# A router product with its operands exchanged: adapter stage of a two-layer mixture-of-experts kernel

## What is computed

```python
# _L0_cond_ref: an adapter chosen by language, then a layer norm
h = relu(einsum('bsh,bha->bsa', x, W1[lang]) + b1[lang])       # a = 64
adapted = einsum('bsa,bah->bsh', h, W2[lang]) + b2[lang]
y = layernorm(x + adapted) * gamma[lang] + beta[lang]
# _L0_ffn_ref: expert-choice routing, 8 experts take 128 of 512 rows each
logits = einsum('bsh,eh->bse', y, Wg)                          # 8 logits a row
Sm = swapaxes(softmax(logits, axis=-1), 1, 2)
G, I = top_k(Sm, 128)
# gather rows I, expert FFN (256 -> 1024 -> 256), scale by G, add back at I
...
```

## Time and profile before

| | us |
|---|---|
| median of three runs | 1123.51 |
| lowest and highest | 1120.33, 1127.12 |
| the profiled execution | 1121.38 |
| its span, first to last instruction | 1119.6 |
| TensorE matmuls busy | 955.4 (85%) |
| TensorE weight loads busy | 680.7 (61%) |
| VectorE busy | 746.9 (67%) |
| ScalarE busy | 460.5 (41%) |
| POOL busy | 662.7 (59%) |
| mean granted clock of TensorE | 0.929 |

### The profile page before, as it was taken

One profiled execution on the slowest core, in us unless ns is written; L12 is line 12 of the kernel. 1 busy time (PEld: TensorE's weight loads), 2 busy tenths in 40 slices (PEclk: granted clock), 3 DMA queues, 4 the chain that ended last, 5 costly groups with the idle time before them and its releaser, 6 DMA issues.

```text
span 1119.6 us, 15008 instructions
## 1 busy us (share of the span) xinstructions
PE 955.4 (85%) x4616; PEld 680.7 (61%) x4616; DVE 746.9 (67%) x1529; ACT 460.5 (41%) x835; POOL 662.7 (59%) x494
## 2 busy tenths in 40 slices
PE   4988899999999999988269889888687799899960
PEld 2664499989998999863125445444454465556640
DVE  3547466666766676524778999999974787777620
ACT  1221354455445554443446565757321232232320
POOL 2113434455544654315999989999940477777870
PEclk9768999999999999998699999999876999999995
DMA  5949534354443442134212832244258599996557
GB/s 177 283 150 343 140 62 95 83 118 93 95 109 88 89 97 45 20 60 110 95 39 77 260 129 89 95 137 129 96 170 296 163 267 269 255 260 154 91 75 155
DMA packets 89783, 155.48 MB, mean 139 GB/s; under 512 B 12072, under 2 KB 70128, under 8 KB 86576
## 3 DMA queue, kind: packets, MB, share of 16 engines
q1 hardware_dynamic: 48112, 91.27, 25.0%
q0 software_dynamic: 25104, 39.86, 20.2%
q10 hardware_dynamic: 16496, 23.49, 6.4%
HBM read 119.56 MB, written 43.42 MB: 146 GB/s over the span
## 4 chain that ended last, share of the span: by engine, by line
issue 12%; POOL 12%; DVE 10%; PE 7%; DMA 6%; DVEq 3%; ACT 1%; POOLq 1%; ACTq 0%
DVE wide L1270 5%; DMA odd_rows<-ys,slots 3%; POOL xg L717 3%; POOL wide L639 2%; PE bank L1656 2%; POOL wide L631 2%; POOL out L724 2%; POOL odd_rows L724 2%; DMA xg<-z_rows,slots 1%; DMA out<-ys,slots 1%; DVEq L1309 1%; PE bank L1733 1%; PE bank L1723 1%; PE bank L1743 1%; ACT wide L891 1%
## 5 line engine op out<-in xcount | busy, mean ns | idle before, releaser
L631 POOL TENSOR_TENSOR wide<-wide 128x1024 f32<-128x1024 f32 x64 | 156.4, 2457 | 30.9 <-issue 30.9
L1270 DVE TENSOR_TENSOR_SCAN wide<-bank,wide 128x512 f32<-128x512 f32 x128 | 149.3, 1210 | 22.7 <-POOL wide L631 22.7
L867 ACT ACTIVATE h_raw<-bank,b 128x512 f32<-128x512 f32 x128 | 87.9, 688 | 168.2 <-PE bank L1629 165.6
L1207 DVE TENSOR_TENSOR h_lo<-h_raw,h_hi 128x512 fp32r<-128x512 f32 x128 | 87.3, 692 | 92.2 <-ACT h_hi L871 88.8
L1644 PE MATMUL bank<-w_hi,h_hi 128*128 128x256 f32 x512 | 144.3, 282 | 0.1
L1644 PE MATMUL bank<-w_hi,h_lo 128*128 128x256 f32 x512 | 142.3, 278 | 0.0
L1644 PE MATMUL bank<-w_lo,h_hi 128*128 128x256 f32 x512 | 142.3, 278 | 0.0
L605 POOL DMA_INDIRECT x_rows<-ob,put x64 | 110.3, 1723 | 28.3 <-issue 16.0
L639 POOL TENSOR_TENSOR wide<-wide 128x1024 f32<-128x1024 f32 x46 | 108.4, 2357 | 11.5 <-issue 8.1
L891 ACT ACTIVATE wide<-wide,blend 128x512 f32<-128x512 f32 x128 | 84.1, 716 | 61.1 <-POOL wide L631 57.4
L1629 PE MATMUL bank<-ex_hi,w_hi 128*128 128x512 f32 x256 | 99.5, 389 | 2.1 <-issue 2.1
(11 more groups left out here) (235 smaller groups left out, 2019.9 us busy)
## 6 DMA issues: line engine op xcount, KB each, us to landing
wide<-in_mwp SPq DMA_DIRECT2D x40, 512.0 KB
wide<-m_rows SPq DMA_DIRECT2D x16, 1024.0 KB, 4.8
w1s<-in_fW SPq DMA_DIRECT2D x8, 1024.0 KB, 5.0
w2s<-in_fW SPq DMA_DIRECT2D x8, 1024.0 KB
own<-in_mwp SPq DMA_DIRECT2D x15, 512.0 KB
z_rows<-zrow SPq DMA_DIRECT2D x8, 640.0 KB, 7.1
head<-in_mwp SPq DMA_DIRECT2D x9, 512.0 KB
xT<-in_xT ACTq DMA_DIRECT2D x8, 512.0 KB, 4.4
```

The costliest lines, as they stand in the source:

```text
L631: G.tensor_tensor(drive[n % DRIVES], gb[d % 2], md[d // HD][:, d % HD, :].unsqueeze(1).to_broadcast([P, CT, S]), ALU.mult).then_inc(c_u, 1)
L867: A.activation(h1_raw[f % 4][:, :], bank[:, 2 + f % 4, :], ACT.Gelu_apprx_tanh, bias=b1_0[:, bass.ds(e, 1), f]).then_inc(b_h, 1)
L1207: V.tensor_tensor(h1_lo[:, f, :], h1_raw[f % 4][:, :], h1_hi[:, f, :].bitcast(F32), ALU.subtract).then_inc(b_lo, 1)
L1270: o = V.tensor_tensor_scan(dst[:, c, :], decay[:, d:d + 1].to_broadcast([P, S]), drive[(D * b + d) % DRIVES][:, c, :], 0.0, ALU.mult, ALU.add)
```

## The change

The router weights become the stationary operand. `wg0` grows to 15 x 8 columns for each column tile, zeros everywhere (two memsets on POOL) but at columns 56 to 63, where the weights are loaded. For batch b a slice of 64 columns is taken so that the 8 weight columns land at partitions 8b to 8b+7 of the output, and the 512 turned rows stream. All eight batches add up in bank 7, 64 partitions by 512 columns; the copies of single batches on VectorE, and TensorE's wait for them (`a_lg`), go. Behind the last batch VectorE copies the 64x512 block to SBUF (into a `y` tile that is no longer used), TensorE turns it with four transposes into bank 6 (128 rows by 4 x 64), and the softmax reads that bank. `lg0` is ordered by tile, then batch, then expert. `k_pT` is raised once more, by these transposes.

```diff
--- before.py
+++ after.py
@@ -97,7 +97,6 @@
         own = sb("own", [P, OWN * WW])
         zeros = own[:, 0:TOK // 4 * H // P]
 
-        wg0 = sb("wg0", [P, CT, E0])
         lang_cols = sb("lang_cols", [P, B, 2 * CT + 1])
         gam0, bet0 = lang_cols[:, :, 0:CT], lang_cols[:, :, CT:2 * CT]
         b1_0 = sb("b1_0", [P, E0, FT0])
@@ -160,7 +159,9 @@
         rstd = [sb(f"rstd{p}", [P, TT]) for p in range(2)]
         nrm = [sb(f"nrm{p}", [P, TT, H]) for p in range(2)]
         yT = sb("yT", [P, CT, S])
-        lg0 = sb("lg0", [P, B, TT, E0])
+        wg0 = sb("wg0", [P, CT, (2 * B - 1) * E0])
+        wg0_at = slice((B - 1) * E0, B * E0)
+        lg0 = sb("lg0", [P, TT, B, E0])
 
         red0 = sb("red0", [P, B * TT])
 
@@ -305,12 +306,12 @@
         a_xin = [sem(f"a_xin{p}", 16) for p in range(2)]
         a_in = [sem(f"a_in{i}", 16 * 3) for i in range(4)]
         a_stored = [sem(f"a_stored{p}", 16) for p in range(2)]
-        a_hm, a_h, a_ad, a_y, a_mv, a_rstd, a_nrm, a_nT, a_yT, a_lgm, a_lg = (
-            sem("a_" + n) for n in ("hm", "h", "ad", "y", "mv", "rstd", "nrm", "nT", "yT", "lgm", "lg"))
+        a_hm, a_h, a_ad, a_y, a_mv, a_rstd, a_nrm, a_nT, a_yT, a_lgm = (
+            sem("a_" + n) for n in ("hm", "h", "ad", "y", "mv", "rstd", "nrm", "nT", "yT", "lgm"))
         credits = [len(credited)]
 
-        k_sub, k_exp, k_prob, k_pT, k_sel, k_idx, k_lists, k_rev, k_tab = (
-            sem("k_" + n, 0) for n in ("sub", "exp", "prob", "pT", "sel", "idx", "lists", "rev", "tab"))
+        k_lT, k_sub, k_exp, k_prob, k_pT, k_sel, k_idx, k_lists, k_rev, k_tab = (
+            sem("k_" + n, 0) for n in ("lT", "sub", "exp", "prob", "pT", "sel", "idx", "lists", "rev", "tab"))
 
         b_w1, b_w2 = sem("b_w1", 16), sem("b_w2", 32)
         b_w1h, b_w1l, b_w2h, b_w2l = sem("b_w1h"), sem("b_w1l"), sem("b_w2h"), sem("b_w2l")
@@ -506,6 +507,9 @@
             G.memset(ident[:, :], 0.0)
             pool.drain()
             G.memset(hT[AD:AD + 1, :], 1.0)
+            pool.drain()
+            G.memset(wg0[:, :, 0:(B - 1) * E0], 0.0)
+            G.memset(wg0[:, :, B * E0:], 0.0)
             pool.drain()
             G.affine_select(out=ident[:, :], in_=ident[:, :], compare_op=ALU.not_equal, fill=1.0, base=0,
                             pattern=[[-1, P]], channel_multiplier=1)
@@ -747,7 +751,7 @@
         def _(act):
             A = nc.scalar
 
-            act.dma_start(wg0[:, :, :], t["fWgT"].rearrange("(c p) e -> p c e", p=P)).then_inc(loaded0, 16)
+            act.dma_start(wg0[:, :, wg0_at], t["fWgT"].rearrange("(c p) e -> p c e", p=P)).then_inc(loaded0, 16)
             act.dma_start(b1_0[:, :, :], t["fb1"]).then_inc(loaded0, 16)
             grant(act, credits[0], credits[1])
 
@@ -1088,10 +1092,6 @@
                                         ALU.subtract, ALU.mult)
                 o.then_inc(a_nrm, 1)
 
-            def a_logits(b):
-                dve.wait_ge(a_lgm, level(b))
-                V.tensor_copy(lg0[:, b, :, :].rearrange("p t e -> p (t e)"), bank[:, 7, 0:TT * E0]).then_inc(a_lg, 1)
-
             def row_bases():
                 dve.wait_ge(consts, 1)
                 V.tensor_scalar(rowbase[:, :], rowbase[:, :], -S, None, ALU.bitwise_and)
@@ -1102,22 +1102,23 @@
                 V.tensor_scalar(rowbase_f[B * E0:P, :], rowbase_f[B * E0:P, :], float(S // 2 - B * S), None, ALU.add)
 
             for b in range(B):
-                if b > 1:
-                    a_logits(b - 2)
                 a_front(b)
                 if b == 2:
                     row_bases()
                 a_norm(b)
-            a_logits(B - 2)
-            a_logits(B - 1)
-
-
-            lgf = lg0[:, :, :, :].rearrange("p b t e -> p (b t) e")
-            rd = red0[:, :].unsqueeze(2).to_broadcast([P, B * TT, E0])
+
+
+            lT = y[(B - 2) % 2][0:B * E0, 0:2, :].rearrange("p t c -> p (t c)")
             dve.drain()
-            V.tensor_reduce(red0[:, :], lgf, AX.X, ALU.max)
+            dve.wait_ge(a_lgm, level(B - 1))
+            V.tensor_copy(lT, bank[0:B * E0, 7, :]).then_inc(k_lT, 1)
+            lgf = lg0[:, :, :, :].rearrange("p t b e -> p (t b) e")
+            lgp0 = bank[:, 6, 0:TT * B * E0].rearrange("p (n e) -> p n e", e=E0)
+            rd = red0[:, :].unsqueeze(2).to_broadcast([P, TT * B, E0])
+            dve.wait_ge(k_pT, 1)
+            V.tensor_reduce(red0[:, :], lgp0, AX.X, ALU.max)
             dve.drain()
-            V.tensor_tensor(lgf, lgf, rd, ALU.subtract)
+            V.tensor_tensor(lgf, lgp0, rd, ALU.subtract)
             dve.drain().then_inc(k_sub, 1)
             dve.wait_ge(k_exp, 1)
             V.tensor_reduce(red0[:, :], lgf, AX.X, ALU.add)
@@ -1125,11 +1126,11 @@
             V.reciprocal(red0[:, :], red0[:, :])
             dve.drain()
             for j in range(TT):
-                V.tensor_tensor(prob[:, j % 2, j // 2, :].rearrange("p (b e) -> p b e", e=E0), lg0[:, :, j, :],
-                                red0[:, :].rearrange("p (b t) -> p b t", t=TT)[:, :, j].unsqueeze(2).to_broadcast([P, B, E0]),
+                V.tensor_tensor(prob[:, j % 2, j // 2, :].rearrange("p (b e) -> p b e", e=E0), lg0[:, j, :, :],
+                                red0[:, j * B:(j + 1) * B].unsqueeze(2).to_broadcast([P, B, E0]),
                                 ALU.mult)
             dve.drain().then_inc(k_prob, 1)
-            dve.wait_ge(k_pT, 1)
+            dve.wait_ge(k_pT, 2)
             V.tensor_copy(ranks[:, :], bank[:, 0, 0:S // 2])
             dve.drain()
             for r in range(K0 // 8):
@@ -1564,11 +1565,9 @@
 
             def a_logits(b):
                 pe.wait_ge(a_yT, level(b))
-                pe.wait_ge(a_lg, level(b - 1))
-                for j in range(TT):
-                    for c in range(CT):
-                        o = T.matmul(bank[:, 7, j * E0:(j + 1) * E0], yT[:, c, j * P:(j + 1) * P], wg0[:, c, :],
-                                     start=(c == 0), stop=(c == CT - 1))
+                for c in range(CT):
+                    o = T.matmul(bank[0:B * E0, 7, :], wg0[:, c, (B - 1 - b) * E0:(2 * B - 1 - b) * E0], yT[:, c, :],
+                                 start=(b == 0 and c == 0), stop=(b == B - 1 and c == CT - 1))
                 o.then_inc(a_lgm, 1)
 
             for b in range(B):
@@ -1582,6 +1581,13 @@
             a_backT(B - 1)
             a_logits(B - 1)
 
+
+            pe.wait_ge(k_lT, 1)
+            for j in range(TT):
+                o = T.transpose(bank[:, 6, j * B * E0:(j + 1) * B * E0],
+                                y[(B - 2) % 2][0:B * E0, 0:2, :].rearrange("p t c -> p (t c)")[:, j * P:(j + 1) * P],
+                                ident[0:B * E0, 0:B * E0])
+            o.then_inc(k_pT, 1)
 
             pe.wait_ge(consts, 1)
             pe.wait_ge(k_prob, 1)
```

## The result

| | before | after |
|---|---|---|
| median of 20 runs each, us | 1125.76 | 1119.36 |
| lowest and highest | 1120.33, 1134.83 | 1115.04, 1126.66 |
| profiled execution, its span | 1121.38, 1119.6 | 1116.69, 1114.9 |

The ratio of the times is 0.9953, with a 95% interval of 0.9935 to 0.9971: the changed kernel is faster by 5.3 us, between 3.3 and 7.3 (the means of the two columns of runs differ by 5.3, the medians by 6.4). Forecast was 8.1 us, and 1115 for the time. The time lies in the range given, but the gain was put too high, outside that interval. The median before, 1123.51 of three runs, became 1125.76 with twenty.

The account below looks back on a forecast made before the run. The prediction took TensorE, partly at low clock, to pace the adapter stage ahead of a dependent chain. Terms -8.1 - 1.5 + 1.5 = -8.1 us, from the 1123.5 median to 1115; 8-in-10 range 1109 to 1124.

Parts of the forecast that it names:

- the middle: Adapter stage, third to last hidden product: clock stays at 1.00, five periods of 6.48 us, 32.4 instead of 40.46, 8.1 less.
- the tail: Last hidden product to end of last logits: 18.9 us instead of 20.4, 1.5 less; bounds nothing and 4.0 gained.
- the new steps: Between last logits and first softmax reduction: PSUM copy, four transposes and two engine waits, +1.1 to +1.8 us, taken as +1.5.
- what is won before the chain's head is won at the end: Time saved ahead of the first expert-layer product shortens the whole kernel equally, as no load in between is late.
- Part 1: Eight logits groups replaced by streaming products: by work alone -0.1 to +0.1 us in each batch, taken as zero.
- rival D: New logits group takes 0.9 us, less than the existing fp32 product shows; 2.4 us gained in all, 1113; chance 0.01.
- Rival A: Adapter-stage clock is not set by what the logits stream and falls as before; 1123 to 1125 us; chance 0.21.
- Rival C: Mostly zero stationary block keeps TensorE at the low level for the whole middle, +15 us, 1139; chance 0.04.
- Rival B: Middle of the adapter stage becomes bound by loads, one or two stalls of 2 us, 1119 to 1120; chance 0.09.
- the remark on the xt loads: Queue of adapter-stage input loads is close: slowest landed after 9.8 us, and a period of 6.48 leaves about 10.

Follow-up runs that it names:

- a_dip: Changed kernel plus one useless 512-column product in TensorE's wait before the transposes of batch 0; ratio to before 0.9971 (0.9939 to 1.0002).
- b_fill1: Kernel before plus one useless 512-column product behind the logits of each of batches 0 to 5; ratio to before 1.0004 (0.9974 to 1.0034).
- a_tail: Changed kernel plus one useless product in each of TensorE's three waits at the end of the adapter stage; ratio to before 0.9962 (0.9939 to 0.9985).
- a_fill: Changed kernel plus useless products in all TensorE waits of the adapter stage, four of them ahead of it; median 1113.47 us of 6 runs, ratio to before 0.9879.
- a_late: Changed kernel plus 60 useless products ahead of the first hidden product; ratio to before 1.0408 (1.0373 to 1.0443).
- b_again: Kernel before, unchanged, run and traced a second time; ratio to before 0.9985 (0.9955 to 1.0014).
- b_again2: Kernel before, unchanged, a third trace; first expert product at 129.21 us, 995.3 us from there to the end; no ratio given.
- a_again: Changed kernel, not altered further, measured and traced a second time; ratio to before 0.9956 (0.9938 to 0.9974).
- a_again2: Changed kernel, not altered further, a third trace; first expert product at 119.84 us, 995.5 us from there to the end; no ratio given.
- b_tail: Kernel before, old logits kept, plus three useless products in TensorE's waits at the end of the adapter stage; ratio to before 0.9993 (0.9960 to 1.0027).

## Why the prediction was right or wrong

The cause was right and the gain too high, 8.1 us against 5.3. By the heads the kernel gained 7.6, near the forecast, but in part by luck: the term that failed, the middle, was 1.9 us too good, and the tail and the new steps together came out 1.4 us better than their terms. The other 2.3 us went missing between the head and the end. That "what is won before the chain's head is won at the end" is thus neither shown nor refuted for so small a gain, and this part of the shortfall stays open.

- **The middle** was right in its cause, and 1.9 us too good in size: -8.1 forecast, -6.2 measured by the start of the last hidden product (65.3 us before, 59.1 after, means of three traces). The step that failed is "I expect the clock, at 1.00 in the batch from 24.86, to stay there until hidden(7) at least". It was taken from one trace, and the term was given no bound of its own. The first batches hold waits that the change does not touch, and the clock was low for one product or two there in each trace of the changed kernel: a dip at 25 us, behind such a wait, in two, a late rise in one. What makes the rise late was not tested. A low hidden product costs 1.7 us. With the wait filled (a_dip) the term came out as computed, 32.13 against 32.4. Two of the three traces of before had no such dip; the third had it at 25 us. Two readings in the working were coarse. The trace of before has four falls, not two, at about 35.6, 45.8, 56.1 and 69.8 us, and none is right at the end of a logits group: each came 0.6 to 1.6 us into the adapted product behind it. The two that the prediction leaves out, with the columns of rows 2:

```profile
45.75:46.00 0.25, 0.25 (x3) 0.22 (x2) 0.00 (x0) 0.00 (x0) 0.00 (x0) 0.77 1.03 426
...
56.00:56.25 0.25, 0.25 (x3) 0.19 (x2) 0.00 (x0) 0.00 (x0) 0.00 (x0) 0.75 0.73 168
```

  So the position of the falls says little. It is b_fill1 that ties them to the mix of work.
- **Part 1** was right: nothing by work alone. 1.81 us before and after from start to next start. With that **rival D**, four rows in 0.9 us, did not come either.
- **The tail** was right with its bounds: -1.5 forecast, -2.4 measured (20.0 to 17.6, means of three). The last logits ran low in two traces and high, at 1.93 us, in the third, where those of batch 6 were low instead. The last transposes were put at 1.7 to 2.1 us and took 1.1 to 1.2, since the clock was up for most or all of them. The eight took 1.04 us at full clock and 1.91 at the low level (batch from 31.30 of before, at 37.88), so they too run at the level that is granted. Its sum for a tail at full clock, 16.4 us, is what a_tail, a_fill and a_fill_b took (16.3).
- **The new steps** were right, a little dear: +1.5 forecast, +1.0 measured (0.32 to 1.35); the handovers were at the lower bound. The sum of the terms measured: -6.2 - 2.4 + 1.0 = -7.6 at the head.
- **The sum set against one execution.** The profiled execution of before took 1121.38, and I moved only to the median of three. The median of twenty is 1125.76, and the part behind the head was 2 to 8 us shorter in it than in most later traces. The absolute figure of 1115 was low for this reason as much as for the middle. The part behind the head moved with it where the shift was large (a_late); its scatter, 8 us, was not in the working.
- **Rival A** is excluded by the batches at 1.00 and by b_fill1. **Rival C** did not come: with the block of 56 zero columns and 8 weights in every batch the clock stayed at 1.00 from about 29 us to the tail. **Rival B** was right in small. In the kernel after, the addition of batch 6 waited for its load, and then the transposes of batch 6 waited for VectorE:

```profile
59.19 1.22 DVE L1076 TENSOR_TENSOR y<-bank,xt 128x1024 f32<-128x1024 f32 x1 [1.00 <-DMA xt<-in_x]
...
65.36 1.09 PE L1563 MATMUL bank<-ident,nrm 128*128 128x128 f32 x8 [0.53 <-DVE nrm L1091]
```

The slowest load took 10.3 us to land. The loads did not get slower for it, since b_again and b_again2 have slowest ones of 10.2 and 10.3 beside the 9.8 of the first trace. At the short period such a load is just too long, as the remark on the xt loads feared. VectorE waited 1.00 us for it here, 0.60 in a_again and 0.82 in a_again2, and TensorE then 0.53 us, not at all, and 0.35 us.

## What to carry to other kernels

Where TensorE is full and its clock is low in some repetitions of the same work, look at what it streams: exchanging operands so that long rows stream, or even adding useless products, can shorten a stage in which no instruction became cheaper (that the added products shorten the whole kernel was not shown for the kernel before). Cost such a change from the same work at both clock levels, and look at the waits ahead of the stretch too, since in the changed kernel the stretch began at the high level wherever its wait was filled, and low in five of six traces where it was not. And set a small gain against several traces of the kernel before; a single execution can be off by more than the gain, in a part that has nothing to do with it.

## What the runs showed of the hardware that was not expected

- Removing nothing and adding a product of 512 columns to each of five batches made their stretch 3.9 us shorter than in the first trace of before, at a clock of 1.00 instead of 0.79 (b_fill1); the shortest stretch without added products was 37.19 us (b_tail), still 0.7 longer.
- A stage with the same program can have its low stretches at different places in two executions: in the first trace of before the clock fell at about 36, 46 and 56 us (the earlier trace rows and the two rows further up); in b_again the third hidden product, at 25 us, was already low, at 3.40 us. The stretch took nearly the same in these two, 40.46 and 40.08 us, but 37.19 in b_tail, in which the work of the stretch is unchanged too.
- At the start of a trace the granted clock reads 1.00 before the first change is recorded, though products there ran at half speed: in a_again2 the stretch to 26.91 reads 1.00 with a hidden product of 3.68 us in it. The durations decide.
